# Half of the attention-output loads move from SyncE's DMA queue to GpSimd's, in a kernel with one core per sequence

## What is computed

```python
xn = _layernorm(x)
qkv = xn @ qkv_w.T + qkv_b                       # 16 heads of 64
logits = q @ k.T / SCALE - softplus(decay_alpha) * |i - j|
s = (softmax(logits) @ v) @ out_w.T + out_b      # the output projection
h = gelu(ternary_linear(xn, w_up))               # weights -1, 0, 1; input over its rms
g = silu(ternary_linear(h, w_down))
return x + s * g
```

## Time and profile before

| | us |
|---|---|
| median of two timed runs | 5820.52 |
| the two timed runs | 5708.48 and 5932.56 |
| the profiled execution, its own time | 5635.6 |
| its span, slowest core (core 6) | 5634.0 |
| spans of the eight cores | 5612.7 to 5634.0 |
| mean granted TensorE clock | 0.829 to 0.832 |

### The profile page before, as it was taken

One profiled execution on the slowest core, in us unless ns is written; L12 is line 12 of the kernel. 1 busy time (PEld: TensorE's weight loads), 2 busy tenths in 40 slices (PEclk: granted clock), 3 DMA queues, 4 the chain that ended last, 5 costly groups with the idle time before them and its releaser, 6 DMA issues.

```text
span 5634.0 us, 42225 instructions; the slowest of 8 cores (5612.7 to 5634.0 us)
## 1 busy us (share of the span) xinstructions
PE 3791.4 (67%) x14646; PEld 1246.5 (22%) x14646; DVE 1031.4 (18%) x1457; ACT 1182.8 (21%) x1427; POOL 309.3 (5%) x580
## 2 busy tenths in 40 slices
PE   4296776766767757667667677284666666648887
PEld 0042222221221212122112222131222222213333
DVE  1511111112111122222222121110111111111111
ACT  1200331322312213323223132000222222210000
POOL 0000000000000000000000000000111111110000
PEclk9597887888888878888778888697889898978888
DMA  1100110111100001101111010112000000023332
GB/s 60 34 1 15 38 40 23 40 30 31 40 23 21 4 17 55 50 30 55 37 42 56 30 41 4 60 62 94 31 30 31 30 31 29 30 85 106 105 107 99
DMA packets 94487, 246.34 MB, mean 44 GB/s; under 512 B 17950, under 2 KB 17966, under 8 KB 86598
## 3 DMA queue, kind: packets, MB, share of 16 engines
q1 hardware_dynamic: 65670, 167.82, 9.4%
q0 software_dynamic: 28608, 75.81, 4.0%
HBM read 167.79 MB, written 75.50 MB: 43 GB/s over the span
## 4 chain that ended last, share of the span: by engine, by line
PE 65%; DMA 10%; DVE 10%; ACT 7%; issue 6%; SPq 1%; ACTq 0%; DVEq 0%; POOLq 0%; POOL 0%
PE ps L809 17%; PE ps L1014 5%; PE ps L1016 5%; PE ps L1118 4%; PE ps L1120 4%; PE ps L777 3%; PE ps L796 3%; DMA attn_scr<-pt 3%; PE ps L1039 2%; PE ps L559 2%; PE ps L561 2%; PE ps L563 2%; PE ps L779 2%; PE ps L778 2%; DVE pt L868 2%
## 5 line engine op out<-in xcount | busy, mean ns | idle before, releaser
L809 PE MATMUL ps<-pt,v_hat 128*65 128x512 f32 x2048 | 978.3, 624 | 0.0
L838 ACT ACTIVATE pt<-ps,negc 128x2048 f32<-128x2048 f32 x256 | 503.6, 1967 | 1116.8 <-PE ps L796 741.2
L1014 PE MATMUL ps<-xn_hi,wt_up 128*128 128x512 bf16 x1024 | 456.0, 445 | 53.5 <-DMA wt_up<-wup_t_scr 50.5
L1118 PE MATMUL ps<-h_ahi,wt_dn 128*128 128x512 bf16 x1024 | 392.2, 383 | 131.2 <-DMA h_alo<-h_scr_lo 131.2
L777 PE MATMUL ps<-q_hi,k_hi 64*128 64x512 bf16 x1024 | 220.1, 425 | 351.0 <-ACT pt L838 344.4
L1016 PE MATMUL ps<-xn_lo,wt_up 128*128 128x512 bf16 x1024 | 452.4, 442 | 0.0
L1039 PE MATMUL ps<-h2b,ones_row 128*1 128x512 f32 x256 | 134.2, 605 | 400.7 <-ACT h2b L1036 400.7
L809 PEld LDWEIGHTS ps<-pt,v_hat 128*65 128x65 f32 x2048 | 275.5, 144 | 560.7 <-issue 560.7
L1120 PE MATMUL ps<-h_alo,wt_dn 128*128 128x512 bf16 x1024 | 391.7, 383 | 0.0
L1025 ACT ACTIVATE hful<-hpre 128x512 f32<-128x512 f32 x128 | 80.5, 629 | 817.8 <-DVE hpre L1021 817.8
L1021 DVE TENSOR_TENSOR hpre<-ps,rfb 128x512 f32<-128x512 f32 x128 | 88.5, 692 | 750.8 <-PE ps L1016 750.8
(11 more groups left out here) (215 smaller groups left out, 3726.4 us busy)
## 6 DMA issues: line engine op xcount, KB each, us to landing
wstg<-wup_in SPq DMA_DIRECT2D x128, 256.0 KB, 2.6
wstg<-wdn_in SPq DMA_DIRECT2D x128, 256.0 KB, 2.6
h_scr_hi<-hhi POOLq DMA_DIRECT2D x128, 128.0 KB, 2.0
h_scr_lo<-hlo POOLq DMA_DIRECT2D x128, 128.0 KB, 2.0
h_ahi<-h_scr_hi SPq DMA_DIRECT2D x16, 1024.0 KB, 16.6
h_alo<-h_scr_lo SPq DMA_DIRECT2D x16, 1024.0 KB, 18.6
x_res<-x_in SPq DMA_DIRECT2D x8, 1024.0 KB, 16.3
attn_scr<-pt POOLq DMA_DIRECT2D x64, 128.0 KB, 2.2
```

The source lines that it names most:

```text
L809: c.inc(te.matmul(ps[0:65, b * 512:(b + 1) * 512], vrr[:, kc, h, 0:65], ptb[:, pcol:pcol + 512], start=(kc == 0), stop=(kc == KC - 1)), "p ...
L838: c.inc(sc.activation(ptb, ps[0:128, 0:2048], AF.Exp, bias=negc[:, 0:1]), "exp")
L1014: c.inc(te.matmul(ps[0:128, b * 512:(b + 1) * 512], wt, xh, start=(dc == 0), stop=False), "up_mm0")
L1118: c.inc(te.matmul(ps[0:128, b * 512:(b + 1) * 512], wt, hh, start=(hc == 0), stop=False), "dn_mm0")
```

## The change

The loads of `attn_f` are dealt out by the chunk `dc`: chunks 0, 2, 4 and 6 stay with SyncE, chunks 1, 3, 5 and 7 go to GpSimd, with a semaphore of their own, `d_afB`. Both go through `dinc`, so either engine waits for each of its loads to land. ScalarE waits for both. SyncE's wait on `c_sp` stays; GpSimd gets no wait of its own ahead of its loads. In the source GpSimd's loads of a block stand ahead of GpSimd's wait for that block's copies and its eight stores, and behind the eight stores of the block before.

```diff
-        *[f"wv{l}" for l in "ABCDEFGH"], "wkA", "wkB", "wqA", "wqB"}
+        *[f"wv{l}" for l in "ABCDEFGH"], "wkA", "wkB", "wqA", "wqB", "d_afB"}
@@
     for qb in range(QB):
         c.wait(sy, "c_sp", c.val("c_sp"))
         for dc in range(DC):
-            c.dinc(sy.dma_start(out=attn_f[0:64, dc * 512:(dc + 1) * 512],
-                                in_=attn_scr[2 * dc, qb]), "d_af")
-            c.dinc(sy.dma_start(out=attn_f[64:128, dc * 512:(dc + 1) * 512],
-                                in_=attn_scr[2 * dc + 1, qb]), "d_af")
+            eng, tg = (sy, "d_af") if dc % 2 == 0 else (gp, "d_afB")
+            c.dinc(eng.dma_start(out=attn_f[0:64, dc * 512:(dc + 1) * 512],
+                                 in_=attn_scr[2 * dc, qb]), tg)
+            c.dinc(eng.dma_start(out=attn_f[64:128, dc * 512:(dc + 1) * 512],
+                                 in_=attn_scr[2 * dc + 1, qb]), tg)
         c.wait(sc, "d_af")
+        c.wait(sc, "d_afB", c.val("d_afB"))
         c.wait(sc, "s_mm", c.val("s_mm"))
```

## The result

The changed kernel is **slower by 2.1%**: ratio of its time to that of the kernel before 1.0212, 95% interval 1.0166 to 1.0258. The median of 11 runs is 5793.6 us (lowest 5762.1); that of 10 runs of the kernel before, the two known ahead among them, is 5691.1 us (lowest 5640.8). Some executions of either kernel run with a lower granted clock on one die and take longer; the ratio leaves them out. The interval has the line of 2% inside, so that the kernel is slower is measured, but not that it is slower by more than 2%. The prediction had 5816 us, range 5734 to 5948, and argued for a rise of 108 us or 1.9%; it gave "within 2%" 0.53 and "slower" 0.44.

A forecast was written before the change was run, and what follows sets the result against it. Stages wait for each other; in stage C block 0 waits for loads, blocks 1 to 3 for GpSimd's stores. Terms of -20.0, +1, +124.2 and +2.9 gave +108 us; added to 5708.5, 5816 us, range 5734 to 5948.

The forecast's parts named there:

- the sum for stage C: Stage C's predicted change: -20.0, +1, +124.2 and +2.9 us, giving +108 us, between +98 and +128.
- The term at nothing: Stage D1's own length: predicted not to change, D1 only shifted whole by what stage C gains or loses.
- signs named ahead: Stage C timeline: L939 of blocks 1 to 3 released by GpSimd's loads 46 us after the last copy started, among others.
- Contention that eats block 0's gain: Rival, block 0: GpSimd's loads and SyncE's work slow each other, gaining nothing; 5836 us, +2.3%; chance 0.06.
- Loads that stay hidden: Rival, blocks 1 to 3: loads land before TensorE ends the previous block; 5684 us, -0.4%; chance 0.05.
- Loads much dearer than stores: Rival, GpSimd's loads: pitch p at 3.6 us or above, loss +127 us or more, 5835 us up; chance 0.06.
- Block 0: Stage C's first block: L939 starts at 3597.6 instead of 3617.6, -20.0 us, with +1 us for contention with `out_w`.
- The pitch p: GpSimd's loads, blocks 1 to 3: 2.8 us from one load's start to the next, bounds 2.54 and 3.47.
- The restart: Blocks 1 to 3, L939 to last copy: 57.44 us from block 0; TensorE's cold start between 0 and 1 us dearer.
- The stores: GpSimd's eight stores ahead of its loads in blocks 1 to 3: 8 x 2.88 = 23.0 us.
- The odd row: Block 0's fourth store, starting 5.70 us after the third instead of 2.86; assumed to happen once more, +2.9 us.
- My line at 2%: Whole kernel: the limit for telling a change from none, +113 us of the profiled time, +116 of the median.

## Why the prediction was right or wrong

**Which step failed.** The mechanism and the sum for stage C held; the step from the sum to the number failed, and a term that stood at nothing. "What is timed is likelier to resemble a timed run, so my number is the lower of them plus the sum" put the base at 5708.5, and 5708.5 + 108 = 5816 lies 4.5 us below the median of 5820.5 that the text gives for the kernel before: as a number it says no change, while the text argues for +1.9%. Measured was a rise of 2.1%. The term at nothing is D1: "whatever it gains or loses there shifts D1 and D2 whole" left no room for D1's own length, and D1 grew by 5.8 us.

**What bounds the stage, and where the loads would land: right.** Most signs named ahead were there: L941 of blocks 1 to 3 released by GpSimd's loads 47 to 48 us after the last copy (46 predicted), TensorE no longer the releaser, VectorE's stall gone, SyncE's loads where they were, L1005 at 4000.75 on a core that entered stage C 5.4 us later than the earlier trace rows's (3994 + 5 = 3999 predicted). Two were not. GpSimd's eight loads of block 0 took 28 us instead of 22, with the late row among them and a pitch mostly above 3 beside the loads of `out_w`; they are hidden there and cost nothing. And D1 changed in length, which the prediction had named as a sign of being wrong. The order of GpSimd's queue is the cause, shown by moving the loads with only the wait that they need.

**The rivals.** Contention that eats block 0's gain: refuted by the split of block 0 alone, and again with ScalarE's queue. Loads that stay hidden: refuted by the trace. Loads much dearer than stores: not at 3.6, but dearer than I took, below.

**The terms, core 6 of before against core 2 of after.** Block 0: 82.2 to 62.0, -20.3 (predicted -20 + 1). On the mean of the cores it is only -18.0, as the first `attn_f` load starts 43.7 us after the stage does instead of 41.8: contention with `out_w` is 1.9, inside my 0 to 2. Blocks 1 to 3: last copy to last copy 105.17, 105.77 and 106.03, sum 317.0, where I had 310.8 + 2.9:

- *The pitch p, the term that was most mis-sized.* Loads from first start to L941: 23.1, 23.2 and 23.8, where 8 x 2.8 - 0.5 = 21.9 was predicted. That is p = 2.95 to 3.03 and +4.4 us over three blocks. I went by the nearest row, a store of the same shape (2.76), and a load is 0.2 dearer. The estimate from the Trainium skill, DMA: Bandwidth & Descriptors, Specifications (p = 2.94), was nearer, though the skill's split of 0.6 and 1 us itself is shown by no row.
- *The restart:* L941 to last copy 58.08 instead of block 0's 57.44, +1.9 over three, inside the 0 to 1 each that I had named and then left out of the sum.
- *The stores:* 68.9 instead of 69.1.
- *The odd row:* I charged 2.9 us for its happening again in the open. It did not: it is tied to a place in GpSimd's sequence of DMAs, and that place is now in block 0's hidden loads. So this term was wrong, by -2.9, and it hid most of the error of p: that the sum came out within 3 us of stage C is in part luck. It also means that the change moved a cost out of the open, which belongs to its gain.

Together stage C is +109.6 on these two cores and +111.1 on the mean; +108 was predicted.

**D1, the term at nothing.** D1 is 5.8 us longer. Its mean is 1157.1 to 1159.9 in the seven traces with `attn_f` loads on GpSimd (1157.1 for the split of blocks 1 to 3, 1159.8 for the changed kernel), and 1153.5 to 1155.2 in the six with neither these nor loads on ScalarE. It does not come from loads that are late, for it is there when stage C is shorter than before (1159.0 and 1158.0), and not from the places of the late rows.

The traces do show where the 5.8 us lie: in TensorE's granted clock, which goes back and forth between 2.4 and 1.2 GHz all through D1. The time at 1.2 GHz adds up to 286.2 us before and 297.5 after (means over eight cores), and half of the difference is 5.7 us. It is 285.9 to 287.7 us in the six traces and 291.2 to 297.5 in the seven. D1 without what the clock took, which is each stretch times the share of the clock not granted in it, is 1010.9 us before, 1011.1 after, and 1009.9 to 1012.2 in all thirteen. So D1's work takes what it took, at a clock that is lower for more of the time. Why loads on GpSimd, long over by then, go with more of it stays open.

**The number and the chances.** 108 us were right to some 3 us in stage C, and with D1 and the rest the rise of the mean span is 116 of 5626, 2.1%. My line at 2% stood 5 us above my sum, and the errors of the sum (3) and of D1 (6) together carried the result over it. Since the measured interval, 1.7 to 2.6%, has the line inside, 0.53 against 0.44 can't be called right or wrong by it. The base can. Ten runs of before have their median at 5691.1 and four of them lie between 5640.8 and 5646.9, so the profiled execution (5635.6) was the sound base and 5708.5 was not; 5635.6 + 108 = 5744 is to be held against the changed kernel's lowest of 5762.1, 0.3% off. That 5816 lies within 0.4% of the median of the eleven runs (5793.6) is luck.

## What to carry to other kernels

When work is moved to another engine's queue, the first question is what stands ahead of it there: GpSimd's eight loads cost nothing ahead of its wait and stores, and 44 us a block behind them. Where each DMA is waited for on its issuing queue, a second queue halves the wait, but so does leaving out the wait, without a new order to get wrong (without the waits eight loads took 6.4 us instead of 23.1). A predicted rise should be given against one base, and that base named with it.

## What the runs showed of the hardware

- GpSimd's DMAs have late starts at fixed places of its stream, the same on all eight cores. Counting the engine's rows from the start of the program, without memsets, they are the 131st (14.2 to 14.4 us idle with no releaser shown) and the 256th in all fourteen traces; with the four memsets at the program's start, which the expectations count in, these are the 135th and the 260th. The 256th is late whatever it is, a store in the open, a hidden load or a tiny DMA: 5.1 to 8.2 us idle ahead of it in thirteen traces. In the kernel without waits for the landings it had 2.6 us, where its neighbours have none. Further ones follow 40 to 120 rows apart, at places that differ between kernels. Sixteen memsets ahead of it do not shift the 256th to another DMA, eight DMAs do. I have no cause for them.
- A waited load of 128 KB costs about 3 us from start to start on GpSimd and 2.5 on SyncE; unwaited they follow each other at 0.51 on GpSimd and 0.64 on SyncE. The timeline of SyncE without waits (core 6):

```profile
3580.50 0.58 SPq L933 DMA_DIRECT2D attn_f<-attn_scr  x1
3581.13 0.60 SPq L935 DMA_DIRECT2D attn_f<-attn_scr  x1
3581.77 0.60 SPq L933 DMA_DIRECT2D attn_f<-attn_scr  x1
```
